# A data-dependent fetch of expert weights moves from a register load on the sync engine to an indirect DMA on GpSimd

## The reference

```python
def _L3_ffn_ref(x, base_W, base_b, disc_mu, disc_sigma, down_W, down_b, up_W, up_b, conv_W, conv_b):
    B, T, D, R, E = (32, 128, 128, 64, 8)
    base = jnp.einsum('btd,od->bto', x, base_W) + base_b
    m1 = x.mean(axis=1)
    m2 = (x * x).mean(axis=1)
    inv_var = 1.0 / (disc_sigma * disc_sigma)
    losses = (jnp.einsum('bd,ed->eb', m2, inv_var) - 2.0 * jnp.einsum('bd,ed->eb', m1, disc_mu * inv_var)
              + jnp.sum(disc_mu * disc_mu * inv_var, axis=1)[:, None]) / D
    idx = jnp.argmin(losses, axis=0)
    Wd, bd = (down_W[idx], down_b[idx])     # and Wu, bu and Wc, bc in the same way
    h = jax.nn.relu(jnp.einsum('btd,bdr->btr', x, Wd) + bd[:, None, :])
    a = jnp.einsum('btr,brd->btd', h, Wu) + bu[:, None, :]
    y = jnp.einsum('btd,bod->bto', a, Wc) + bc[:, None, :]
    return base + y
# in reference():
    x = x + _L3_ffn_ref(_layernorm(x, axis=-1), ...)
```

## Time and profile before

| | us |
|---|---|
| runs | 6372.74, 6373.38, 8482.34 |
| median of the runs | 6373.38 |
| span of the profiled execution | 6377.2 |
| TensorE busy in it | 5660.4 |
| VectorE busy in it | 4083.4 |
| ACT busy in it | 2814.7 |
| GpSimd busy in it | 2033.5 |

### The profile page before, as it was taken

One profiled execution on the slowest core, in us unless ns is written; L12 is line 12 of the kernel. 1 busy time (PEld: TensorE's weight loads), 2 busy tenths in 40 slices (PEclk: granted clock), 3 DMA queues, 4 the chain that ended last, 5 costly groups with the idle time before them and its releaser, 6 DMA issues. The chain is left out here.

```text
span 6377.2 us, 121100 instructions
## 1 busy us (share of the span) xinstructions
PE 5660.4 (89%) x38029; PEld 3501.2 (55%) x38029; DVE 4083.4 (64%) x9620; ACT 2814.7 (44%) x4608; POOL 2033.5 (32%) x2936
## 2 busy tenths in 40 slices
PE   7997999999996999979987998899998989876677
PEld 5664444444443777457754776467754556534464
DVE  7885666666664776367744775377736656577764
ACT  4553222222221555435553555445555645433344
POOL 5551000000001665156623664166620012241012
PEclk9998999999998999989998999899999999987799
DMA  4332332222224555055513553065500000000002
GB/s 131 111 102 95 97 97 96 98 96 96 97 97 106 152 150 136 1 142 150 150 46 85 152 150 103 21 157 150 152 9 5 0 6 0 1 4 0 0 2 61
DMA packets 526325, 526.98 MB, mean 83 GB/s; under 512 B 55698, under 2 KB 436705, under 8 KB 503780
## 3 DMA queue, kind: packets, MB, share of 16 engines
q1 hardware_dynamic: 517684, 517.90, 29.3%
q10 hardware_dynamic: 8320, 5.25, 0.3%
HBM read 337.88 MB, written 185.07 MB: 82 GB/s over the span
## 5 line engine op out<-in xcount | busy, mean ns | idle before, releaser
L361 DVE TENSOR_REDUCE a_mx<-a_unit 128x2 f32<-128x512 f32 (+1 forms) x1920 | 1297.6, 688 | 608.3 <-PE a_unit L556 600.1
L460 ACT ACTIVATE a_prob<-a_slot 128x1536 f32<-128x1536 f32 x640 | 928.4, 1451 | 732.8 <-PE a_slot L579 571.0
L554 PE MATMUL a_unit<-a_sk,a_sq 96*128 96x256 bf16 (+3 forms) x5120 | 746.9, 250 | 87.4 <-DVE a_mx L361 43.9
L1169 ACT ACTIVATE f_silu<-f_pG 128x512 f32<-128x512 f32 x528 | 314.8, 598 | 935.0 <-PE f_pG L1244 920.9
L556 PE MATMUL a_unit<-a_maskq,identb 128*128 128x256 bf16 (+1 forms) x1920 | 601.7, 313 | 0.0
L1111 DVE TENSOR_TENSOR f_gated<-f_spread,f_silu 128x512 f32<-128x512 f32 x512 | 354.5, 692 | 349.1 <-ACT f_silu L1169 309.0
L1221 PE MATMUL f_pO<-f_hidden,f_wd 128*128 128x512 f32 x1056 | 545.6, 599 | 13.0 <-DVE f_hidden L1113 12.9
L1244 PE MATMUL f_pG<-f_xnT,f_wg 128*128 128x512 f32 x1056 | 543.1, 596 | 0.0
L554 PEld LDWEIGHTS a_unit<-a_sk,a_sq 96*128 96x128 bf16 (+1 forms) x5120 | 383.0, 99 | 289.3 <-DVE a_mx L361 159.5
L1248 PE MATMUL f_pU<-f_xnT,f_wu 128*128 128x512 f32 x1056 | 540.9, 594 | 0.0
L602 PE MATMUL a_pctx<-a_prob,a_vaug 128*32 128x256 f32 x5120 | 423.4, 392 | 89.3 <-POOL a_prob L307 85.1
(11 more groups left out here) (407 smaller groups left out, 10942.6 us busy)
## 6 DMA issues: line engine op xcount, KB each, us to landing
f_spread<-f_scratch SPq DMA_DIRECT2D x1024, 128.0 KB, 2.9
a_sq<-a_qscratch SPq DMA_DIRECT2D x128, 768.0 KB, 5.7
a_sk<-a_kscratch SPq DMA_DIRECT2D x160, 384.0 KB, 6.6
a_qscratch<-a_parts SPq DMA_DIRECT2D x288, 192.0 KB, 2.2
a_qscratch<-a_parts SPq DMA_DIRECT2D x288, 128.0 KB, 2.2
a_kscratch<-a_parts SPq DMA_DIRECT2D x160, 192.0 KB, 2.2
a_kscratch<-a_parts SPq DMA_DIRECT2D x160, 128.0 KB, 2.2
a_qscratch<-a_parts SPq DMA_DIRECT2D x288, 64.0 KB, 1.8
```

Source lines behind the costliest of these rows:

```text
L361: v.tensor_reduce(dst, src, op=ALU.max, axis=AX.X, negate=True).then_inc(red_done, 1)
L460: act.activation(prob[gr % 2][:, :], slot[:, :], ACT.Exp, scale=SCALE).then_inc(exp_done, 1)
L554: pe.matmul(bank[:, at * wide:(at + 1) * wide], q, sk[b][0:KM, gr * GH + h, 0:wide], start=(at == 0), stop=False)
L1169: act.activation(silu[c % 2][:, :], pG[c % 2][:, :], ACT.Silu).then_inc(silu_done, 1)
```

## The change

VectorE no longer leaves one index on one partition. TensorE makes the losses on all 128 partitions (the sums are broadcast as 128 columns of weights, `length` becomes 128x128), so gain, max and find index run on 128 partitions. VectorE then converts the index to float and forms for each partition the row `128 * index + partition` of the table seen as 1024 rows, using a new constant `lane` (loaded with a fifth DMA at the stage's start), into one of two `row` buffers, after a wait for the fetch that used that buffer. GpSimd issues the fetch as an indirect DMA, one row to each partition, in its step between outb and rstd. SP keeps only the stores.

```diff
--- before.py
+++ after.py
@@ -2237,13 +2237,14 @@
         base = k.sb("base", [P, D]); baseb = k.sb("baseb", [P, 1])
         mu = k.sb("mu", [P, E]); sigma = k.sb("sigma", [P, E]); var = k.sb("var", [P, E]); iv = k.sb("iv", [P, E])
         muiv = k.sb("muiv", [P, E]); cross = k.sb("cross", [P, E]); square = k.sb("square", [P, E])
-        length = k.sb("length", [P, 1]); mhalf = k.sb("mhalf", [P, QT])
+        length = k.sb("length", [P, P]); lane = k.sb("lane", [P, 1]); mhalf = k.sb("mhalf", [P, QT])
         stats = k.sb("stats", [P, QT, 6]); moments = k.sb("moments", [P, QT, 2])
         veps = k.sb("veps", [P, QT]); rstd = k.sb("rstd", [P, QT])
         xn = k.sb("xn", [P, QT, D]); xnT = [k.sb(f"xnT{b}", [P, SEQ]) for b in range(4)]; sqr = k.sb("sqr", [P, SEQ])
         sum1 = k.sb("sum1", [P, 1]); sum2 = k.sb("sum2", [P, 1])
-        gain = k.sb("gain", [1, E]); best = k.sb("best", [1, E])
-        at = [k.sb(f"at{b}", [1, E], mybir.dt.uint32) for b in range(4)]
+        gain = k.sb("gain", [P, E]); best = k.sb("best", [P, E])
+        at = k.sb("at", [P, E], mybir.dt.uint32); choice = k.sb("choice", [P, 1])
+        row = [k.sb(f"row{b}", [P, 1], mybir.dt.uint32) for b in range(2)]
         mine = [k.sb(f"mine{b}", [P, W]) for b in range(4)]; outb = [k.sb(f"outb{b}", [P, 1]) for b in range(4)]
         hT = k.sb("hT", [R, SEQ]); aT = k.sb("aT", [P, SEQ]); yT = k.sb("yT", [P, SEQ])
         pT = k.ps("pT", [P, BLK]); pL = k.ps("pL", [P, BLK]); pH = k.ps("pH", [P, BLK]); pA = k.ps("pA", [P, BLK])
@@ -2253,7 +2254,8 @@
             "w_in setup disc_done apart aside stats_done rstd_done xn_done t_pe xnT_done sq_done l_pe picked "
             "outb_done h_pe hT_done a_pe aT_done y_pe yT_done r_pe x_done put")
         loaded = [k.sem(f"loaded{b}") for b in range(4)]
-        W_IN = 16 * 4
+        W_IN = 16 * 5
+        table = w["every"].rearrange("e p c -> (e p) c")
 
         def used(i, j, ahead):
 
@@ -2262,21 +2264,12 @@
         with nc.Block() as block:
             @block.sync
             def _(sp):
-                for dst, src in ((mu, w["mu"]), (sigma, w["sigma"]), (base, w["base"]), (baseb, w["baseb"])):
+                for dst, src in ((mu, w["mu"]), (sigma, w["sigma"]), (base, w["base"]), (baseb, w["baseb"]),
+                                 (lane, core["lane"])):
                     sp.dma_start(dst[:, :], src).then_inc(w_in, 16)
 
                 def step(i, j):
                     n = i * 4 + j
-                    if is_seq(n + 3):
-                        b = (j + 3) % 4
-                        sp.wait_ge(picked, n + 4)
-                        sp.sem_inc(aside, 1)
-                        choice = sp.value_load(at[b][0:1, 0:1], min_val=0, max_val=E - 1)
-                        if is_seq(n - 1):
-                            sp.sem_inc(aside, 1)
-                            sp.wait_ge(yT_done, n)
-                        sp.dma_start(mine[b][:, :], w["every"][bass.ds(choice, 1), :, :].rearrange("e p c -> p (e c)")
-                                     ).then_inc(loaded[b], 16)
                     if is_seq(n - 2):
                         sp.sem_inc(aside, 1)
                         sp.wait_ge(x_done, n - 1)
@@ -2303,6 +2296,16 @@
                         if is_seq(n - 3):
                             g.wait_ge(yT_done, n - 2)
                         g.tensor_tensor(outb[b][:, :], mine[b][:, BC:BC + 1], baseb[:, :], op=ALU.add).then_inc(outb_done, 1)
+                    if is_seq(n + 3):
+                        b = (j + 3) % 4
+                        g.wait_ge(picked, n + 4)
+                        if is_seq(n - 1):
+                            g.sem_inc(apart, 1)
+                            g.wait_ge(yT_done, n)
+                        g.sem_inc(apart, 1)
+                        g.indirect_dma_start(mine[b][:, :], None, table,
+                                             bass.IndirectOffsetOnAxis(row[(j + 1) % 2][:, 0:1], 0)
+                                             ).then_inc(loaded[b], 16)
                     if is_seq(n + 5):
                         g.wait_ge(stats_done, n + 6)
                         ln_rstd(g, chain, moments, veps, mhalf, rstd, 1e-5, rstd_done, apart)
@@ -2330,9 +2333,14 @@
                         ln_apply(v, rows(core["x"], (n + 4) * QT, QT), moments, rstd, xn).then_inc(xn_done, 1)
                     if is_seq(n + 3):
                         v.wait_ge(l_pe, n + 4)
-                        link(v.tensor_scalar(gain[:, :], pL[0:1, 0:E], -1.0 / (D * SEQ), None, ALU.mult))
+                        link(v.tensor_scalar(gain[:, :], pL[:, 0:E], -1.0 / (D * SEQ), None, ALU.mult))
                         link(v.max(best[:, :], gain[:, :]))
-                        v.max_index(at[(j + 3) % 4][:, :], best[:, :], gain[:, :]).then_inc(picked, 1)
+                        link(v.max_index(at[:, :], best[:, :], gain[:, :]))
+                        link(v.tensor_copy(choice[:, :], at[:, 0:1]))
+                        if is_seq(n + 1):
+                            v.wait_ge(loaded[(j + 1) % 4], used(i, j, 1))
+                        v.scalar_tensor_tensor(out=row[(j + 1) % 2][:, :], in0=choice[:, :], scalar=float(P), in1=lane[:, :],
+                                               op0=ALU.mult, op1=ALU.add).then_inc(picked, 1)
                     if is_seq(n - 1):
                         dst = rows(core["x"], (n - 1) * QT, QT)
                         v.wait_ge(r_pe, n)
@@ -2396,9 +2404,9 @@
                         pe.wait_ge(sq_done, n + 4)
                         if is_seq(n + 2):
                             pe.wait_ge(picked, n + 3)
-                        pe.matmul(pL[0:1, 0:E], sum2[:, :], iv[:, :], start=True, stop=False)
-                        pe.matmul(pL[0:1, 0:E], sum1[:, :], cross[:, :], start=False, stop=False)
-                        pe.matmul(pL[0:1, 0:E], length[:, :], square[:, :], start=False, stop=True).then_inc(l_pe, 1)
+                        pe.matmul(pL[:, 0:E], sum2[:, :].broadcast_to((P, P)), iv[:, :], start=True, stop=False)
+                        pe.matmul(pL[:, 0:E], sum1[:, :].broadcast_to((P, P)), cross[:, :], start=False, stop=False)
+                        pe.matmul(pL[:, 0:E], length[:, :], square[:, :], start=False, stop=True).then_inc(l_pe, 1)
                     if is_seq(n + 1):
                         b = (j + 1) % 4
                         pe.wait_ge(loaded[b], used(i, j, 1))
@@ -2661,7 +2669,7 @@
     core["ident"], core["identb"] = pool("ident", [P, P])[:, :], pool("identb", [P, P], BF16)[:, :]
     core["mean"], core["rstd"] = pool("row_mean", [P, TILES]), pool("row_rstd", [P, TILES])
     core["arriving"] = Arriving(nc, core, a)
-    for name in ("maskq", "maskk", "ones2", "esel", "turn", "kturn", "tri", "selhm", "sell", "diag", "iota8"):
+    for name in ("maskq", "maskk", "ones2", "esel", "turn", "kturn", "tri", "selhm", "sell", "diag", "iota8", "lane"):
         core[name] = a[name]
     return core
 
@@ -2692,6 +2700,7 @@
     c["kturn"] = np.concatenate([parts[i] for i in KPART])
     c["ones2"] = b16(np.ones((2, HEADS, SEQ), np.float32))
     c["diag"] = np.kron(np.eye(GH, dtype=np.float32), np.ones((32, 9), np.float32))
+    c["lane"] = np.arange(P, dtype=np.float32)[:, None]
     c["iota8"] = np.arange(8, dtype=np.float32)[None]
     c["tri"] = np.tril(np.ones((8, 8), np.float32), -1).reshape(64)
     sel = np.zeros((64, 32, 128), np.float32)
```

## The result

The changed kernel takes 6461.66, 6462.10 and 6450.99 us, the kernel before 6372.74, 6373.38 and 6379.45 us: ratio 1.013, 95% interval 1.0116 to 1.0144. It is slower by some 83 us, within the 2% that I had given 0.96, but far beyond the forecast of 6391 and the range up to 6428. (One execution of each kernel was disturbed, 19254.39 and 8482.34 us, with a granted clock of 0.348 in that of the changed one; they are left out.)

A forecast was written before the change was run, and what follows sets the result against it. The loop of VectorE and GpSimd through rstd was taken to set the pace, 3.97 us a step. Terms 11.5 + 1.4 + 0 + 3.0 + 0.4 + 0.9 + 0.5 = 17.7 us on the median 6373.38 gave 6391 us, range 6378 to 6428.

The forecast's parts named there:

- VectorE's term, 12.9 us: VectorE's added drains, copy, multiply-add and register wait lie in the loop: 0.46 plus 0.07 us, 11.5 + 1.4 us in total.
- GpSimd, "exposed 0": GpSimd's gather ahead of veps and rstd: taken as 1.4 us, hidden by a cover of 1.40 us, costing 0.
- the upper bound of 2.5 us: GpSimd's gather: at most a landing of 2.2 plus an issue of 0.34 us, costing 27.5 us.
- my terms for the ramp: First steps: +3.0 us for TensorE's wide loads, +0.4 for loading lane, +0.9 for the later first fetch.
- the 0.65 that I had named as a sign of being wrong: Steady loop: the prediction is wrong if the period moves by under 0.3 or over 0.65 us.
- A later landing hurts nobody, as there are 8 us: Fetch: used two steps, some 8 us, after issue, so a later landing costs nothing in steady state.
- TensorE, hidden in steady state, +3.0 in the ramp: Six 128-column weight loads: +0.43 us a step within slack of 1.08; exposed in three low-clock ramp steps, +3.0 us.
- `lane`, +0.4 in the ramp: Stage start: a fifth load on SP's queue, for which everything waits, costs one more issue, +0.4 us.
- Rival (c): Nothing shows: VectorE's part at its low 7.5 us, ramp loads free, 0.4 for lane; 6381 us, chance 0.14.
- Rival (a): GpSimd's gather outlasts its cover and joins the loop, delaying veps; 6391 to 6421 us, middle 6405, chance 0.26.
- Rival (b): Gather descriptors can't be written while VectorE works, exposing its whole 1.4 us a step; 6426 us, chance 0.07.
- (d): Gather holds GpSimd over 5.8 us, stretching the loop 4.4 us more per step; slower by over 2%, chance 0.03.

The follow-up runs named there:

- e11: Kernel before, with VectorE's stats of sequence n+5 moved ahead of the argmax and residual add, and a drain added: 6363.0 us, ratio 0.9974.
- e6: Kernel before plus only VectorE's added drains, copy, wait and multiply-add, on one partition, result unused, SP fetching as before: 6391.1 us, ratio 1.0022.
- e4: Changed kernel with a plain GpSimd DMA of the same size, always adapter 0, in place of the gather: 6447.4 us, ratio 1.0108.
- e9: Changed kernel with rstd ahead of the gather, a semaphore replacing its drain, and row numbers made on GpSimd behind rstd: 6406.7 us, ratio 1.0046.
- e5: Kernel before with only TensorE's 128-column weight loads for the losses; VectorE reads partition 0, SP fetches as before: 6384.4 us, ratio 1.001.
- e10: Kernel before with only the fetch changed to GpSimd's gather ahead of rstd, with fixed row numbers (adapter 0): 6452.8 us, ratio 1.0114.
- e2: Changed kernel, same order, with a semaphore raised by veps in place of the drain between veps and rstd: 6421.0 us, ratio 1.0073.
- e3: Changed kernel without the gather: wide losses and VectorE's added operations kept, SP fetching as before: 6416.3 us, ratio 1.0064.
- e1: Changed kernel with veps, drain and rstd of sequence n+5 moved ahead of the gather on GpSimd: 6406.5 us, ratio 1.005.

## Why the prediction was wrong

- **What bounds the kernel** (right). The loop of VectorE and GpSimd set the pace; the changed one's loss lies wholly in it, and e11, which shortens only that loop, is faster.
- **VectorE's term, 12.9 us** (right). e6 alone costs 15 us and 0.52 us a step; in the changed kernel find to copy is 0.24, copy to multiply-add 0.30, multiply-add to residual add 0.23.
- **GpSimd, "exposed 0"** (the step that failed). I priced the gather as an instruction, 1.4 us against a cover of 1.40; its row is 1.08 us. Three things were wrong round it. First and largest, I let veps and rstd follow at their old distance, 0.37 us, and didn't ask what the drain between them would now wait for. The list of what stands behind the new instruction on its engine had veps and rstd in it, but not the drain: 1.76 us a step, of the 2.80 by which the step grew. Second, the start: 0.99 us after the row numbers, where I took 0.26 from the distance of a semaphore; this exposes 0.42 us a step. What fills the 0.99 us no run takes apart; the plain DMA of e4 starts after 0.77. Third, the upper bound of 2.5 us used SP's landing of 2.2 us; GpSimd's gather lands in 3.0. That bound did describe what happened, GpSimd held until the landing, and I named it only as a bound and charged it against the cover. At 0.42 + 1.76 = 2.18 us, 25 steps give 54 us more, and 31 steps 68; added to my 17.7 that gives 72 to 85, where 82.7 (span) were measured. By place: the last 25 steps cost 69 us more than before, 2.8 each, and the first six 14 us, where my terms for the ramp came to 4.3. The steady period moved by 2.7 us, far over the 0.65 that I had named as a sign of being wrong.
- **"A later landing hurts nobody, as there are 8 us"** (wrong twice). The drain made the loop wait for it, and the fetch of the earlier trace rows, issued at 6298.85, is used by the pH after the next one, about 4.3 us later, not 8: I counted the offset of the steps without seeing that TensorE runs one step ahead. e9 fell into that.
- **TensorE, hidden in steady state, +3.0 in the ramp** (half right). e5 costs 8 us and only in the ramp, so the term's place was right and its size short by 5. But I held the clock at 1.00. In e6, e10 and the changed kernel, whose steps are longer, it was lower: 0.88, 0.63 and 0.50. That the wide loads are then no longer hidden shows in the steps of 6.2 to 6.4 us of e2; for e3's 40 us, against 8 and 15 for its parts, it is inferred.
- **`lane`, +0.4 in the ramp** (right). The first veps starts 4.05 us after the stage's first load, 3.66 before. (Rival (c) calls this 0.5 in its words and adds 0.4.)
- **Rival (a)** named the right place (GpSimd's veps and rstd become late, the loop takes it up) but its price ended at 1.1 us a step; the measured one is 2.2. **Rival (b)** is out: the gather starts while VectorE's stats run (6334.85 against 6334.55). That this case shows no such stall agrees with the Trainium skill (SBUF — State Buffer, Who interferes with whom), by whose list an instruction of VectorE with one SBUF input, outside the 2-port modes, doesn't contend with GpSimd; the stats and the moments, which run beside the gather here, have one input each and are not among the operations that it names for those modes. **(c)** and **(d)** didn't occur: the step grew by 2.7 us, and (d) wanted 4.4 on top of 0.5.
- By the Trainium skill (DMA: Bandwidth & Descriptors, Latency and other measured facts) the first byte comes after about 1 us from GpSimd and 0.6 from SP, 0.4 us apart, an estimate from that page. No run here shows a first byte. The landings differ by 0.8 us here (3.0 against 2.2), and the issue itself holds the engine for 1.08 us against 0.34.

## What to carry to other kernels

When a DMA is moved to an engine that computes, look for the drains behind it on that engine and not only for the instructions: here a drain 1.1 us behind the DMA waited for the landing and cost four times what the DMA's own exposure did. Put the work that others wait for ahead of the DMA, or order it by a semaphore of its own; the first gave back some 53 of the 83 us (e1), the second some 38 (e2). And don't take slack on TensorE at the high clock for granted when the change lengthens the loop round it: check whether the work still fits at the lower level.

## What the runs showed of the hardware

- What stands behind a drain on GpSimd starts 0.1 to 0.2 us after GpSimd's last DMA has landed, in all 120 cases: 3.25 us after the DMA's start at a landing of 3.1, 4.57 at 4.4, 3.02 at 2.8 (plain DMA), 2.56 at 2.4 (small gather). A semaphore from the operation itself doesn't wait for it: 1.45 us after the start.
- A gather of 128 rows holds GpSimd 1.08 us, whether the rows are of 323 or of 16 numbers (1.08 to 1.14 in e1); a plain DMA of the same size as the 323 0.60; the first one 1.23 and 0.80. Where the wait for the row numbers ends last, the gather of the changed kernel starts 0.8 to 1.0 us later (the plain DMA 0.6 to 0.8); where they are long ready (e1), 0.2 to 0.3 us after rstd's end.
- TensorE's granted clock was 1.00 in the steady steps of the kernel before and 0.63 in e10, where TensorE has the same work and idles some 1.4 us a step behind the stall instead of 0.6; in the changed kernel it stayed at 0.50 (the 1.2 GHz level) with TensorE at work for 31.20 of 32 us, and in e5 at 1.00 (2.4 GHz) with 38.29 of 40. Why the one stays low and the other high is open.
